# Shifted window attention: heads in four groups of three, first heads turned behind the projection, values and weighted values in 32-column tiles

## The chip, the cores and the metric

The kernel runs on one core of one Trainium2 chip. The metric is the device time of one execution in microseconds. Engines are called as in the profile: PE (matrix products and transposes), DVE (vector), ACT (scalar), POOL and SP (which issues most DMAs). Everything is fp32.

## The reference, cut to what matters

The input is 32 images of 96 channels by 16 x 16 positions. Two blocks follow each other; the change is in the first half of the first, the shifted window attention:

```python
xn = layernorm(x, norm1_g, norm1_b)                    # over the 96 channels of a position
xw = windows(roll(xn, (-4, -4)))                       # 4 windows of 8 x 8 = 64 positions per image
q, k, v = split(xw @ qkv_w + qkv_b)                    # 12 heads of 8 channels each
attn = softmax(q * 8**-0.5 @ k.T + rel_bias + mask)    # 64 x 64 per window and head
out = (attn @ v) @ proj_w + proj_b
x = x + unroll(out)                                    # the residual
x = x + gelu(layernorm(x) @ fc1_w + fc1_b) @ fc2_w + fc2_b
```

Then comes a second block (whole-image normalisation, grouped pointwise and 3 x 3 depthwise convolutions, attention between the 12 channels of a head, a final projection). The feed-forward part and the second block are the same before and after.

## The kernel before

Function `window_attention` works through the images one by one, and every engine runs its own program: a loop over steps, each with an order written out by hand, in which stages of several images stand together. In step t the engines work on images t to t + 4. `led_image_loop` runs four steps ahead of image 0, then the steps 0 to 31, in a loop of two steps per lap in the middle, and one step more behind the last image. Engines wait for each other by counting semaphores.

The stages of an image, in the order of its life:

- `turn_tokens` (PE): two transposes of the loaded image into `ps_tokens`, 128 positions a time. `measure` and `gather_spread` (DVE) take mean and variance, `inverse_deviation` and `scale` (ACT) scale the tokens, `turn_back` (PE) transposes them back into `ps_scaled`, `copy_normed` (ACT) copies them to `normed` in the order of the windows.
- `make_q_and_k` (PE): two products of 256 columns. `copy_q` (ACT) adds the bias. `copy_k` (DVE) adds the bias and spreads the keys into `k_blocks`: the keys once for each head of a group, with all channels but those of that head set to zero by `head_mask`. Heads stand in three groups (`NG`) of four (`GROUP`), 32 channels a group.
- `make_v` (PE): per window two products of 64 rows of output (64 columns of the array), `copy_v` (ACT) copies them to `v_blocks`, where each head has a ninth column of ones.
- For each of the two pairs of windows (p = 0, 1): `score` (PE) multiplies 64 queries with 256 columns of `k_blocks`, three groups and two windows; `add_bias` and `find_peak` (DVE); `subtract_peak` (POOL); `exponent` (ACT); `turn` (PE), six transposes; `copy_turned` (ACT).
- `weigh` (PE): probabilities times values, 12 products with 64 columns of the array and 54 moving columns: 18 are those of two heads, and the 36 behind them are written again by the next products (the last ones meet zero columns kept for this). The ones give the sum. `weigh_heads` (DVE) divides, `turn_heads` (PE) transposes, `copy_ot` (ACT) copies to `out_t`.
- `project` (PE) and `add_residual` (DVE), into `stream`.

The order in step t on PE is: project(t-1), turn_heads(t, 0), make_q_and_k(t+2), weigh(t, 1), turn(t+1, 0), score(t+2, 0), turn_heads(t, 1), turn_back(t+3), make_v(t+2), weigh(t+1, 0), score(t+2, 1), turn_tokens(t+4), turn(t+1, 1). On DVE: gather_spread, copy_k(t+2), weigh_heads(t, 1), add_residual(t-1), add_bias and find_peak(t+2, 0), weigh_heads(t+1, 0), add_bias(t+2, 1), measure(t+4), find_peak(t+2, 1). On ACT: copy_ot(t, 0), exponent(t+1, 0), copy_q(t+2), inverse_deviation and scale(t+3), copy_turned(t+1, 0), copy_ot(t, 1), exponent(t+1, 1), copy_normed(t+3), copy_v(t+2), copy_turned(t+1, 1).

PSUM has eight banks: three for the scores (q and k lie behind the scores of groups 0 and 1), two for the turned probabilities, one for the weighted values and turned heads (`ps_out`), `ps_a` for tokens and scaled tokens, `ps_b` for values and projection.

Ahead of the loop DVE and PE fold the norm's gain and bias into the weights (`prepare`, `fold_q_k_v`); PE runs products of zeros between (`fill`). SP loads the constants in two lists. In the last steps the tokens of the first eight chunks of the feed-forward part are turned (`turn_first`).

## Time and profile before

| | us |
|---|---|
| median of 3 timed runs (lowest, highest) | 508.53 (503.3, 512.01) |
| the profiled execution's own time | 499.01 |
| its span, first to last instruction | 497.2 |
| busy in the span: PE, DVE, ACT, POOL | 481.4, 369.7, 293.8, 195.7 |
| granted TensorE clock, mean | 0.994 |

The profiled execution is a single one, and its time is lower than the three timed runs. Busy times overlap. A PE that counts as busy need not be at its peak, since matmuls are pipelined and their ends are modelled. In the rows, "x24" is the count of instructions merged into one row, and an fp32 product counts as two matmuls, a transpose as one. Row starts are in us from the span's start. PEld are PE's weight loads.

### The profile page before, as it was taken

The page shows a single profiled execution, that of the slowest core. Times are in us where ns is not written, and L with a number is a line of the kernel's source. Part 1 is how long each engine was busy: PE and PEld are TensorE (multiplying, and loading weights), DVE is VectorE, ACT ScalarE, POOL GpSimd, SP SyncE. Part 2 cuts the span into 40 slices and gives each one's busy share as a digit, 9 for nine tenths or more (in the row PEclk, how much of TensorE's full clock was granted, in tenths as well). Part 3 has the DMA queues.
Part 4 walks back from the last instruction along what each step waited for, and adds up shares of the span by engine and source line. Part 5 has one row for each costly group of instructions (what it writes and reads, how often), then busy time and mean ns, then how long its engine had stood idle before and what let it go on. Part 6 is the DMA issues. An engine that isn't in the chain of part 4 may idle for free. (4 is left out here: it accounts for less than half of the span.)

```text
span 497.2 us, 22898 instructions
## 1 busy us (share of the span) xinstructions
PE 481.4 (97%) x8834; PEld 308.6 (62%) x8834; DVE 369.7 (74%) x1013; ACT 293.8 (59%) x743; POOL 195.7 (39%) x238
## 2 busy tenths in 40 slices
PE   8999999999999999999879999989999999999995
PEld 7767777777777777777644443335656565565652
DVE  2699999999999999999875463575765565656453
ACT  2577787778877787777665443433434444444431
POOL 8544434434443434443452542253344323233200
PEclk9999999999999999999999999999999999999999
DMA  4211011111111011100013232386444444443401
GB/s 81 69 36 33 21 28 50 32 24 24 32 32 29 19 32 32 32 16 3 2 40 97 51 81 66 96 213 140 121 116 110 114 120 117 106 123 104 126 21 32
DMA packets 41179, 32.54 MB, mean 65 GB/s; under 512 B 19240, under 2 KB 36776, under 8 KB 41128
## 3 DMA queue, kind: packets, MB, share of 16 engines
q1 hardware_dynamic: 36872, 25.36, 20.0%
q0 software_dynamic: 3584, 5.72, 5.3%
q10 hardware_dynamic: 672, 0.75, 0.5%
q8 instruction: 36, 0.59, 0.5%
q14 instruction: 15, 0.12, 0.1%
HBM read 18.36 MB, written 7.13 MB: 51 GB/s over the span
## 5 line engine op out<-in xcount | busy, mean ns | idle before, releaser
L380 POOL TENSOR_TENSOR scores<-scores,peak 128x768 f32<-128x768 f32 x64 | 94.2, 1472 | 128.3 <-DVE peak L560 128.3
L1043 POOL DMA_DIRECT2D x_stack<-padded_x x96 | 52.3, 548 | 91.9 <-PE ps_hidden L1563 70.6
L443 ACT COPY probs_t<-ps_probs 128x768 f32<-128x768 f32 x64 | 51.1, 798 | 40.4 <-PE ps_probs L707 40.3
L552 DVE TENSOR_TENSOR scores<-ps_scores,bias 128x768 f32<-128x768 f32 x64 | 61.3, 957 | 5.4 <-PE ps_scores L697 3.6
L560 DVE TENSOR_REDUCE peak<-scores 128x12 f32<-128x768 f32 x64 | 61.0, 953 | 2.4
L720 PE MATMUL ps_out<-v_blocks,probs_t 128*64 128x54 f32 x1536 | 57.2, 224 | 1.0 <-ACT out_t L448 0.9
L720 PEld LDWEIGHTS ps_out<-v_blocks,probs_t 128*64 128x64 f32 x1536 | 50.2, 138 | 12.3 <-issue 12.2
L437 ACT ACTIVATE scores<-scores 128x768 f32<-128x768 f32 x64 | 54.2, 847 | 1.5 <-POOL scores L380 1.5
L707 PE MATMUL ps_probs<-ident,scores 128*128 128x128 f32 x384 | 54.3, 277 | 0.0
L1563 PE MATMUL ps_turn<-x_stack,conv_w 40*32 40x256 f32 x1536 | 48.8, 379 | 1.6 <-DMA x_stack<-padded_x 1.6
L1563 PE MATMUL ps_hidden<-x_stack,conv_w 40*32 40x256 f32 x1536 | 49.5, 379 | 0.2 <-issue 0.2
L1151 ACT ACTIVATE hidden<-ps_hidden,fc_b_folded 128x512 f32<-128x512 f32 x44 | 26.6, 688 | 30.1 <-PE ps_hidden L1480 30.1
L697 PE MATMUL ps_scores<-k_blocks,q_sb 32*64 32x256 f32 x768 | 43.1, 399 | 0.9 <-issue 0.9
L707 PEld LDWEIGHTS ps_probs<-ident,scores 128*128 128x128 f32 x384 | 41.6, 140 | 2.8 <-issue 0.8
L539 DVE SCALAR_TENSOR_TENSOR k_blocks<-ps_scores,b_k,head_mask 96x1024 f32<-96x1024 f32 x32 | 40.6, 1269 | 2.5 <-PE ps_scores L675 2.5
L1170 ACT COPY qk_sb<-ps_turn 128x512 f32<-128x512 f32 x32 | 18.7, 586 | 38.4 <-PE ps_turn L1563 38.4
L1563 PEld LDWEIGHTS ps_turn<-x_stack,conv_w 40*32 40x32 f32 x1536 | 26.2, 105 | 21.5 <-issue 14.2
L1406 DVE TENSOR_REDUCE peak<-ps_hidden 128x2 f32<-128x24 f32 x32 | 5.8, 183 | 40.2 <-PE ps_hidden L1593 40.2
L1480 PE MATMUL ps_hidden<-normed,fc_sliced 32*128 32x512 f32 x264 | 31.4, 604 | 2.1 <-PEq L149 1.7
L1175 ACT COPY v_sb<-ps_hidden 128x512 f32<-128x512 f32 x32 | 18.8, 586 | 23.9 <-PE ps_hidden L1563 23.9
L1496 PE MATMUL ps_y<-hidden,fc 128*32 128x512 f32 x288 | 32.8, 595 | 0.0
L1563 PEld LDWEIGHTS ps_hidden<-x_stack,conv_w 40*32 40x32 f32 x1536 | 26.7, 105 | 8.6 <-issue 0.7
(157 smaller groups left out, 847.6 us busy)
## 6 DMA issues: line engine op xcount, KB each, us to landing
x_stack<-padded_x POOLq DMA_DIRECT2D x96, 54.0 KB, 2.7
x_stack<-padded_x SPq DMA_DIRECT2D x96, 54.0 KB
padded_x<-x_pad SPq DMA_DIRECT2D x26, 121.5 KB, 2.6
x_sliced<-stream SPq DMA_DIRECT2D x48, 64.0 KB, 2.0
stream<-y_sliced SPq DMA_DIRECT2D x48, 64.0 KB, 2.1
out<-out_sb SPq DMA_DIRECT2D x32, 96.0 KB, 2.0
x_now<-in_x SPq DMA_DIRECT2D x32, 72.0 KB, 1.8
stream<-in_x SPq DMA_DIRECT2D x32, 72.0 KB, 1.9
```

Source lines behind the costliest of these rows:

```text
L380: nc.gpsimd.tensor_tensor(sc, sc, peak[:, par, p, :].unsqueeze(2).to_broadcast((128, HEADS, WN)), ALU.subtract).then_inc(s["shifted"], 1)
L437: nc.scalar.activation(scores[:, par, p, :], scores[:, par, p, :], ACT.Exp).then_inc(s["probs_ready"], 1)
L443: nc.scalar.copy(probs_t[:, :], ps_turned).then_inc(s["turned_copied"], 1)
L539: nc.vector.scalar_tensor_tensor(out=k_blocks[:, :, :], in0=ps_k.unsqueeze(1).to_broadcast((C, GROUP, N)), scalar=b_k[:, 0:1], in1=head_ma ...
L552: nc.vector.tensor_tensor(scores[:, par, p, :].rearrange("p (g c) -> p g c", g=NG), ps_scores[:, :, 0:GROUP * WN], bias[:, p, :].rearrange ...
L560: nc.vector.tensor_reduce(peak[:, par, p, :], scores[:, par, p, :].rearrange("p (h m) -> p h m", m=WN), AX_X, ALU.max).then_inc(s["peak_re ...
L697: mm = nc.tensor.matmul(ps_scores[64 * w:64 * w + 64, g, 0:GROUP * WN], q, k, start=True, stop=True, skip_group_check=True)
L707: mm = nc.tensor.transpose(ps_turned[:, q * 128:(q + 1) * 128], scores[:, par, p, q * 128:(q + 1) * 128], ident[:, :])
L720: mm = nc.tensor.matmul(ps_out[64 * top:64 * top + 64, 0, q * 2 * VC:(q + 3) * 2 * VC], probs_t[:, q * 128 + 64 * top:q * 128 + 64 * top + ...
L1043: engine.dma_start(x_stack[64 * half + i * HC:64 * half + (i + 1) * HC, slot, :, :], rows).then_inc(landed[slot], 16)
L1496: mm = nc.tensor.matmul(ps_y[32 * r:32 * r + 32, n % 2, :], w["fc2"][:, h, 32 * c:32 * c + 32], hidden[:, g % 2, r, h, :], start=(h == 0), ...
L1563: mm = nc.tensor.matmul(ps[32 * k:32 * k + 32, r, :], conv_w[rows, kind, j, k, :], grid(x_stack[rows, slot, k, :], PADW)[:, :, j:j + W], s ...
```

## The change

- Heads stand in four groups of three. A group has 24 channels, padded to 32 rows with zeros (`w_qk`, `b_q`, `b_k`, `head_mask` and `cols_qk` get the padded form), and the scores have a bank for each of the four groups, 192 columns in each. `copy_k` writes 128 x 768 elements, where it wrote 96 x 1024.
- Tokens, scaled tokens, values and projection share one bank, `ps_ab`: tokens and values one region, scaled tokens and projection the other. New waits keep them apart: `turn_tokens` waits for copy_v of the image before, `turn_back` for a residual, `project` for copy_normed.
- `make_v` and `weigh` use tiles of 32 columns of the array: four products where two stood. `weigh` moves 18 columns, without the 36 that were written again, and `v_blocks` loses its zero columns.
- project(t) and turn_heads(t+1, 0) stand at the end of step t, ahead of turn_tokens(t+4) and turn(t+1, 1), where they stood behind these at the start of the next step. copy_ot(t+1, 0) goes ahead of copy_turned(t+1, 1) on ACT; add_residual(t) goes between measure(t+4) and find_peak(t+2, 1) on DVE. The step behind the last image is dropped.
- In the setup three loads leave SP's first list, eight small ones are issued by ACT ahead of its table load, behind two clears by POOL. The folded weights are copied by two instructions, and the folded biases of q and k are made group by group (`fold_q_k_v`, not shown).

```diff
...
-GROUP = 4
+GROUP = 3
+GROUP_C = GROUP * HD
+GROUP_COLS = GROUP * WN
...
-    step(B, B // 2, 0)
 def image_loop(engine, step, tail=1, lead=1, between=None, start=0):
...
-    head_mask = sb("head_mask", [C, GROUP])
+    head_mask = sb("head_mask", [128, GROUP])
-    w_qkv = sb("w_qkv", [C, 3 * C])
+    w_qk = sb("w_qk", [C, 2, NG, 32])
+    w_v = sb("w_v", [C, C])
-    b_q = sb("b_q", [C, 1])
-    b_k = sb("b_k", [C, 1])
+    cols_qk = sb("cols_qk", [128, 2])
+    b_q = sb("b_q", [128, 1])
+    b_k = sb("b_k", [128, 1])
...
-    q_sb = sb("q_sb", [C, N])
-    k_blocks = sb("k_blocks", [C, GROUP, N])
-    v_blocks = sb("v_blocks", [128, 2, PAIRS, 2, HP + 2, 2, VC])
+    q_sb = sb("q_sb", [128, N])
+    k_blocks = sb("k_blocks", [128, GROUP, N])
+    v_blocks = sb("v_blocks", [128, 2, PAIRS, 2, HP, 2, VC])
...
-    ps_a = bank("ps_a")
-    ps_b = bank("ps_b")
-    ps_tokens = ps_a[:, 0, 0:2 * C].rearrange("p (h c) -> p h c", c=C)
-    ps_scaled = ps_a[0:C, 0, N:2 * N]
+    ps_ab = bank("ps_ab")
+    ps_tokens = ps_ab[:, 0, 0:2 * C].rearrange("p (h c) -> p h c", c=C)
+    ps_scaled = ps_ab[0:C, 0, 2 * C:2 * C + N]
-    ps_q, ps_k = (ps_scores[0:C, g, GROUP * WN:GROUP * WN + N] for g in range(2))
-    ps_v = ps_b[:, 0, 0:2 * C].rearrange("p (w q d) -> p w q d", w=2 * PAIRS, d=HD)
-    ps_proj = ps_b[0:C, 0, 0:N]
+    ps_q, ps_k = (ps_scores[:, g, GROUP_COLS:GROUP_COLS + N] for g in range(2))
+    ps_v = ps_ab[:, 0, 0:2 * C].rearrange("p (w q d) -> p w q d", w=2 * PAIRS, d=HD)
+    ps_proj = ps_ab[0:C, 0, 2 * C:2 * C + N]
...
-    FIRST, SECOND = 8, 7
+    FIRST, SECOND = 5, 7
+    GROUPED = 2 * NG
...
-                 *((cols[:, 2 + k:3 + k], a["L0_conv_qkv_b"][k * C:(k + 1) * C].rearrange("(c a) -> c a", a=1))
-                   for k in range(3)),
-                 (head_mask[:, :], a["c_head_mask"]))
+                 (cols[:, 4:5], a["L0_conv_qkv_b"][2 * C:3 * C].rearrange("(c a) -> c a", a=1)))
...
     def _(pool):
+        nc.gpsimd.memset(head_mask[:, :], 0.0).then_inc(group_cleared, 1)
+        nc.gpsimd.memset(cols_qk[:, :], 0.0).then_inc(group_cleared, 1)
...
+        act.wait_ge(group_cleared, 2)
+        for g in range(NG):
+            rows, channels = slice(32 * g, 32 * g + GROUP_C), slice(GROUP_C * g, GROUP_C * (g + 1))
+            act.dma_start(cols_qk[rows, :], a["L0_conv_qkv_b"][0:2 * C].rearrange("(k c) -> c k", k=2)[channels, :],
+                          allow_slow_non_contiguous=True).then_inc(grouped_in, 16)
+            act.dma_start(head_mask[rows, :], a["c_head_mask"][0:GROUP_C, 0:GROUP]).then_inc(grouped_in, 16)
         def step(t, half, par):
-            if real(t):
-                copy_ot(t, 0, par)
             if is_image(t, B - 1):
...
             if is_image(t, B - 2):
             if real(t + 1):
+                copy_ot(t + 1, 0, 1 - par)
             if is_image(t, B - 2):
...
-                                    ps_scores[:, :, 0:GROUP * WN],
+                                    ps_scores[:, :, 0:GROUP_COLS],
...
         def add_residual(t, half, par):
-            dve.wait_ge(stream_in[1 - par], half * 32 if par == 0 else (half + 1) * 32)
+            dve.wait_ge(stream_in[par], (half + 1) * 32)
...
-            nc.vector.tensor_tensor(b_q[:, :], ps_out[0:C, 0, 0:1], cols[:, 2:3], ALU.add).then_inc(set_up, 1)
-            nc.vector.tensor_tensor(b_k[:, :], ps_out[0:C, 0, 1:2], cols[:, 3:4], ALU.add).then_inc(set_up, 1)
+            dve.wait_ge(grouped_in, 16 * GROUPED)
+            nc.vector.tensor_tensor(b_q[:, :], ps_out[:, 0, 0:1], cols_qk[:, 0:1], ALU.add).then_inc(set_up, 1)
+            nc.vector.tensor_tensor(b_k[:, :], ps_out[:, 0, 1:2], cols_qk[:, 1:2], ALU.add).then_inc(set_up, 1)
...
+            nc.vector.tensor_copy(w_qk[:, :, :, 0:GROUP_C].rearrange("c k g i -> c (k g) i"),
+                                  ps_folded[:, 0:2 * C].rearrange("c (g i) -> c g i", i=GROUP_C)).then_inc(centred, 1)
+            nc.vector.tensor_copy(w_v[:, :], ps_folded[:, 2 * C:3 * C]).then_inc(centred, 1)
         def step(t, half, par):
             if real(t + 3):
...
             if is_image(t, B - 2):
-            if real(t - 1):
-                add_residual(t - 1, half, par)
             if is_image(t, B - 2):
             if is_image(t, B - 1):
...
             if real(t + 4):
+            if real(t):
+                add_residual(t, half, par)
             if real(t + 2):
+        nc.vector.memset(w_qk[:, :, :, :], 0.0).then_inc(blanked, 1)
...
         def turn_tokens(t, half, par):
-            need(pe, s["scaled_ready"], t * 2)
+            need(pe, s["v_copied"], (t - 1) * 2)
         def turn_back(t):
+            need(pe, s["residual_done"], t - 3)
...
         def make_q_and_k(t):
             if is_image(t, 0):
-                pe.wait_ge(centred, 1)
+                pe.wait_ge(centred, 2)
-            nc.tensor.matmul(ps_q, w_qkv[:, 0:C], normed[:, :], start=True, stop=True,
+            nc.tensor.matmul(ps_q, w_qk[:, 0, :, :].rearrange("c g i -> c (g i)"), normed[:, :], start=True, stop=True,
-            nc.tensor.matmul(ps_k, w_qkv[:, C:2 * C], normed[:, :], start=True, stop=True,
+            nc.tensor.matmul(ps_k, w_qk[:, 1, :, :].rearrange("c g i -> c (g i)"), normed[:, :], start=True, stop=True,
         def make_v(t):
-            heads = w_qkv[:, 2 * C:3 * C].rearrange("c (q e d) -> c q e d", e=2, d=HD)
+            heads = w_v[:, :].rearrange("c (q e d) -> c q e d", e=2, d=HD)
-                for e in range(2):
-                    mm = nc.tensor.matmul(ps_v[64 * e:64 * e + 64, window, :, :], normed[:, window * WN:(window + 1) * WN],
-                                          heads[:, :, e, :], start=True, stop=True, skip_group_check=True)
+                for quarter in range(4):
+                    at = window * WN + 32 * (quarter % 2)
+                    mm = nc.tensor.matmul(ps_v[32 * quarter:32 * quarter + 32, window, :, :], normed[:, at:at + 32],
+                                          heads[:, :, quarter // 2, :], start=True, stop=True, skip_group_check=True)
         def score(t, p):
...
-                    mm = nc.tensor.matmul(ps_scores[64 * w:64 * w + 64, g, 0:GROUP * WN], q, k, start=True, stop=True,
+                    mm = nc.tensor.matmul(ps_scores[64 * w:64 * w + 64, g, 0:GROUP_COLS], q, k, start=True, stop=True,
...
-                for top in range(2):
-                    mm = nc.tensor.matmul(ps_out[64 * top:64 * top + 64, 0, q * 2 * VC:(q + 3) * 2 * VC],
-                                          probs_t[:, q * 128 + 64 * top:q * 128 + 64 * top + 64],
-                                          v_blocks[:, par, p, top, q:q + 3, :, :].rearrange("p q e c -> p (q e c)"),
+                for quarter in range(4):
+                    rows = slice(32 * quarter, 32 * quarter + 32)
+                    mm = nc.tensor.matmul(ps_out[rows, 0, q * 2 * VC:(q + 1) * 2 * VC],
+                                          probs_t[:, q * 128 + 32 * quarter:q * 128 + 32 * quarter + 32],
+                                          v_blocks[:, par, p, quarter // 2, q, :, :].rearrange("p e c -> p (e c)"),
...
         def project(t, par):
+            pe.wait_ge(s["normed_ready"], up_to(t + 3) * PAIRS)
...
         def step(t, half, par):
-            if real(t - 1):
-                project(t - 1, 1 - par)
-            if real(t):
-                turn_heads(t, 0)
             if is_image(t, B - 2):
...
             if real(t + 2):
+            if real(t):
+                project(t, par)
+            if real(t + 1):
+                turn_heads(t + 1, 0)
             if real(t + 4):
             if is_image(t, -3):
```

## Rows read from the trace of the kernel before

**Rows 1.** Windows: length, busy us of PE, PEld, DVE, ACT, POOL (instructions), granted clock, DMA.

```profile
10.00:20.00 10.00, 10.00 (x104) 8.16 (x103) 5.60 (x13) 2.72 (x10) 8.11 (x12) 0.83 0.29 59
100.00:140.00 40.00, 40.00 (x642) 29.43 (x630) 38.64 (x79) 31.78 (x85) 16.20 (x11) 1.00 0.12 28
```

**Rows 2.** Timeline of one step: start us, us, engine, line, operation, [idle before <-releaser].

```profile
160.79 0.85 ACT L437 ACTIVATE scores<-scores 128x768 f32<-128x768 f32 x1
...
161.46 1.26 DVE L539 SCALAR_TENSOR_TENSOR k_blocks<-ps_scores,b_k,head_mask 96x1024 f32<-96x1024 f32 x1
...
162.89 0.67 PE L697 MATMUL ps_scores<-k_blocks,q_sb 32*64 32x256 f32 x12
...
163.00 0.80 ACT L443 COPY probs_t<-ps_probs 128x768 f32<-128x768 f32 x1
163.19 0.48 DVE L577 SCALAR_TENSOR_TENSOR stream<-ps_b,b_proj,stream 96x256 f32 x1
...
163.74 0.96 DVE L552 TENSOR_TENSOR scores<-ps_scores,bias 128x768 f32<-128x768 f32 x1
163.85 0.26 ACT L448 COPY out_t<-ps_out 96x128 f32<-96x128 f32 x1
...
164.46 0.88 PE L720 MATMUL ps_out<-v_blocks,probs_t 128*64 128x54 f32 x24
...
165.05 0.68 ACT L432 COPY v_blocks<-ps_b 64x192 f32<-64x192 f32 x2
...
165.26 0.67 PE L697 MATMUL ps_scores<-k_blocks,q_sb 32*64 32x256 f32 x12
...
165.87 0.39 PE L659 MATMUL ps_a<-ident,x_now 96*128 96x96 f32 x2
...
166.09 0.82 PE L707 MATMUL ps_probs<-ident,scores 128*128 128x128 f32 x6
...
166.75 0.60 PE L736 MATMUL ps_b<-out_t,w_proj 96*96 96x256 f32 x2
166.95 0.80 ACT L443 COPY probs_t<-ps_probs 128x768 f32<-128x768 f32 x1 [1.21 <-PE ps_probs L707]
...
166.99 0.42 DVE L524 BATCH_NORM_STATS2 token_stats<-ps_a 128x6 f32<-128x96 f32 x2
...
167.18 0.27 PE L729 MATMUL ps_out<-ident,heads_out 128*96 128x128 f32 x1
...
167.34 0.59 PE L673 MATMUL ps_scores<-normed,w_qkv 96*96 96x256 f32 x2
...
167.64 0.26 ACT L448 COPY out_t<-ps_out 96x128 f32<-96x128 f32 x1
...
168.50 1.28 DVE L539 SCALAR_TENSOR_TENSOR k_blocks<-ps_scores,b_k,head_mask 96x1024 f32<-96x1024 f32 x1
```

**Rows 3.** Timeline, copies of the keys of images 2 and 31; 28 stand between them.

```profile
27.94 1.25 DVE L539 SCALAR_TENSOR_TENSOR k_blocks<-ps_scores,b_k,head_mask 96x1024 f32<-96x1024 f32 x1
...
231.49 1.28 DVE L539 SCALAR_TENSOR_TENSOR k_blocks<-ps_scores,b_k,head_mask 96x1024 f32<-96x1024 f32 x1 [0.27 <-PE ps_scores L675]
```

**Rows 4.** Groups of instructions, the Gram product: busy us, mean ns of one.

```profile
L1593 PE MATMUL ps_hidden<-tokens 128*32 128x12 f32 x1024 | 14.1, 182 | 0.2 <-DVE tokens L1401 0.2
```

**Rows 5.** Timeline of the drain: a copy by ACT and the product that waits for it.

```profile
243.91 0.27 ACT L448 COPY out_t<-ps_out 96x128 f32<-96x128 f32 x1
...
244.28 0.91 PE L720 MATMUL ps_out<-v_blocks,probs_t 128*64 128x54 f32 x24 [0.93 <-ACT out_t L448]
```

**Rows 6.** Timeline of the setup, 0 to 8 us.

```profile
0.86 1.28 ACT L450 ACT_TABLE_LOAD   x1 [0.86 <-PEq L1682]
...
5.53 0.43 SPq L330 DMA_DIRECT2D head_mask<-in_c_head_mask  x1
5.83 0.30 ACT L398 ACTIVATE log_var<-spread,eps 128x2 f32<-128x2 f32 x1 [3.69 <-DVE spread L534]
...
7.67 0.37 DVE L582 TENSOR_SCALAR w_gained<-w_in,cols 96x288 f32<-96x288 f32 x1 [1.94 <-DMA head_mask<-in_c_head_mask]
```

More of the change, by code:

```diff
@@ L257, in window_attention @@
     ps_ot = ps_out[0:C, 0, 384:512]
-    first_homes = [ps_scores[:, 0, :], ps_scores[:, 1, :], ps_scores[:, 2, :], ps_a[:, 0, :]]
+    first_homes = [ps_scores[:, g, :] for g in range(NG)]
     ps_fold = [ps_probs[:, c % 2, 0:HID] for c in range(SLICES)]
-    ps_fold_b = ps_a[:, 0, BLOCKS * C:BLOCKS * C + HT]
+    ps_fold_b = ps_scores[:, 3, BLOCKS * C:BLOCKS * C + HT]
     ps_slices = [ps_probs[:, 1 - c % 2, :] for c in range(SLICES)]
@@ L265, in window_attention @@
     consts_in = sem("consts_in")
+    group_cleared = sem("group_cleared")
+    grouped_in = sem("grouped_in")
     second_in = sem("second_in")
@@ L538, in copy_k @@
             need(dve, s["scores_ready"], t * 2)
-            nc.vector.scalar_tensor_tensor(out=k_blocks[:, :, :], in0=ps_k.unsqueeze(1).to_broadcast((C, GROUP, N)),
+            nc.vector.scalar_tensor_tensor(out=k_blocks[:, :, :], in0=ps_k.unsqueeze(1).to_broadcast((128, GROUP, N)),
                                            scalar=b_k[:, 0:1],
-                                           in1=head_mask[:, :].unsqueeze(2).to_broadcast((C, GROUP, N)),
+                                           in1=head_mask[:, :].unsqueeze(2).to_broadcast((128, GROUP, N)),
                                            op0=ALU.add, op1=ALU.mult).then_inc(s["k_copied"], 1)
@@ L589, in prepare @@
             dve.wait_ge(folded, 1)
-            nc.vector.tensor_copy(w_qkv[:, :], ps_folded).then_inc(centred, 1)
+            dve.wait_ge(blanked, 2)
+            nc.vector.tensor_copy(w_qk[:, :, :, 0:GROUP_C].rearrange("c k g i -> c (k g) i"),
+                                  ps_folded[:, 0:2 * C].rearrange("c (g i) -> c g i", i=GROUP_C)).then_inc(centred, 1)
+            nc.vector.tensor_copy(w_v[:, :], ps_folded[:, 2 * C:3 * C]).then_inc(centred, 1)
         def step(t, half, par):
@@ L638, in fold_q_k_v @@
             pe.wait_ge(consts_in, 16 * FIRST)
-            for k in range(3):
-                nc.tensor.matmul(ps_out[0:C, 0, k:k + 1], w_in[:, k * C:(k + 1) * C], cols[:, 1:2],
-                                 start=True, stop=True, skip_group_check=True).then_inc(pe_set, 1)
+            for k in range(2):
+                for g in range(NG):
+                    at = k * C + g * GROUP_C
+                    mm = nc.tensor.matmul(ps_out[32 * g:32 * g + 32, 0, k:k + 1], w_in[:, at:at + 32], cols[:, 1:2],
+                                          start=True, stop=True, skip_group_check=True)
+                mm.then_inc(pe_set, 1)
+            nc.tensor.matmul(ps_out[0:C, 0, 2:3], w_in[:, 2 * C:3 * C], cols[:, 1:2],
+                             start=True, stop=True, skip_group_check=True).then_inc(pe_set, 1)
         def fold_v():
```

## The prediction

> **What bounds the kernel now.** I read the windows first. Between 100 and 140 us PE is busy 40.00 of 40 us and DVE 38.64, ACT 31.78, POOL 16.20 [rows 1]. Two engines are full at once, so the share of busy time can't say which one a saving has to come from. The timeline of one step tells more [rows 2]: copy_k of one image starts at 161.46 and of the next at 168.50, so this step takes 7.04 us, and from the copy of image 2 at 27.94 to that of image 31 at 231.49 there are 29 steps of 7.02 us [rows 3]. The change touches these steps, the setup ahead of them and the drain behind; the phases that follow the attention have the same instructions before and after.
>
> In that step the reader is to follow three chains. On PE each group begins when the one before has left the array (score at 162.89, weigh at 164.46, score at 165.26, tokens at 165.87, turn at 166.09, project at 166.75, heads at 167.18, q at 167.34): PE waits for nobody. On DVE the gaps are under 0.1 us: copy_k, reciprocal and weighted heads, residual (163.19), bias (163.74), peak, reciprocal and heads, the second bias, statistics (166.99), peak, spread, copy_k (168.50). ACT runs without a pause from one copy_turned behind the second turn to the end of copy_v at 165.73, and is then idle 1.21 us until turn has given it the next such copy_turned at 166.95.
>
> **The change part by part.**
>
> *32-column tiles on PE.* Weigh goes from 24 matmuls to 48, make_v from 16 to 32, each score from 12 to 16 (an fp32 product is two instructions). Weigh now holds PE from 164.46 to 165.26, 0.80 us, or 33 ns a matmul [rows 2]. The nearest row in the new form is the Gram product of the last phase, 128 rows by 32 columns with 12 moving: 1024 in 14.1 us, 14 ns each [rows 4]. 48 x 14 = 0.66 us, so two weighs give back about 0.3 us, bounds 0 and 0.7 (the upper if four tiles cost what two did: 0.80 / 2 each, with its start). make_v gains the same share of a smaller group, 0.1. A score has 192 moving columns in place of 256 in each of two passes: 64 columns x 2 x 2 passes over 2.4 GHz (the granted clock is 1.00 [rows 1]) is 0.11 us less, 4 matmuls more at the Gram row's 14 ns cost 0.06, so 0.67 becomes about 0.62. In all PE loses some 0.5 to 0.8 us of 7.02 and stops being the bound. Whether that shortens the step depends on who is second, and DVE is 0.25 us behind.
>
> The Trainium skill speaks against this part: "TensorEngine Tiling (Array Packing)", Performance Considerations, says that a matmul has some 60 cycles of overhead, that one moving column costs as much as 60, and that tiling should not be taken from a dimension that is already small; weigh goes from 54 moving columns to 18. By its figure (25 ns at 2.4 GHz, an estimate) a weigh would take 1.2 us. The Gram row is at 14 ns with 12 columns, so the trace does not agree where tiles of one shape follow each other.
>
> *copy_k.* 96x1024 took 1.26 us, and the residual, the same operation on 96x256, 0.48 [rows 2]. On the line through both, 128x768 takes 1.00: 0.26 us less on DVE per step.
>
> *The residual moves.* It runs now between the weighted heads and the bias addition, from 163.19 to 163.67, while DVE waits for the score anyway: the score can start only when copy_k has ended at 162.72, and its result lets the bias start at 163.74. So its 0.48 us is free today. In the change it stands between the statistics and the second peak, where DVE has no wait; there it costs 0.51 (itself and a gap of 0.03). The hole that it leaves stays open: copy_k's end to the score's start is 0.17, the score 0.62, its end to the bias 0.18, together 0.97 in place of 1.02, with almost 0.5 of it idle (reciprocal and heads stay in it).
>
> *DVE's chain, summed.* Now: copy_k 1.26, to the bias 1.02, bias to statistics 3.25 (163.74 to 166.99), statistics to the next copy_k 1.51; together 7.04. After: 1.00 + 0.97 + 3.25 + 1.51 + 0.51 = 7.24. Bounds: with the score at 0.56 (no charge for the four) and its start 0.10 behind copy_k (as short as the wait shown at the drain [rows 5]) it is 7.11; with an unchanged score 7.29.
>
> *One PSUM bank for tokens, values, normalised tokens and projection.* This adds waits. turn_tokens(t+4) waits for copy_v(t+2), since both write one region; project(t) waits for copy_v(t+2) and copy_normed(t+3); turn_back waits for a residual of the step before, which is long done. Today turn_tokens starts at 165.87, only 0.14 us behind copy_v, and the projection stands behind turn. After the change project, turn_heads(t+1, 0), turn_tokens and turn(t+1, 1) queue on PE behind copy_v, and ACT's next work, copy_turned, is behind turn. That closes a loop between ACT and PE, and each link has its price in [rows 2]. ACT: copy_turned to the next exponent 0.69 (166.95 to 167.64; the copy of the first heads that stands there now moves into the idle time ahead of copy_turned); exponent 160.79 to the end of copy_v 165.73, 4.94, of which copy_turned to copy_ot took 0.85 where 0.69 is enough; turn_heads came late there, and with a shorter weigh and score it should not, so 4.78. PE: 0.10 from ACT's end to the matmul [rows 5], project 0.43 (166.75 to 167.18), heads 0.16 (167.18 to q at 167.34), tokens 0.22, turn to copy_turned 0.86 (166.09 to 166.95). Sum 0.69 + 4.78 + 0.10 + 0.43 + 0.16 + 0.22 + 0.86 = 7.24 us. Bounds: 7.15 with the links tighter by what the rows round away, 7.40 if the late turn_heads stays. DVE waits in this loop too: its statistics need the tokens, which come about 1.1 us behind copy_v, where DVE's own chain has it ready at about the same time.
>
> So two chains stand at 7.24, and PE's own work far below. With the same rounding the step shown is 7.04 where the mean is 7.02, so I take 7.22: a step grows by 0.20 us, 29 steps by 5.8.
>
> *Moved copy_ot and turn_heads.* The first heads are turned earlier and copied in ACT's idle time, so weigh(t, 1) no longer waits for them. PE's queue was full then, so this is worth nothing by itself. The cover is ACT's wait for turn, some 1.7 us after the change; without it 0.16 would return.
>
> *Setup.* Three DMAs leave SP's first list. Each holds SP 0.43 us and a small gap (head_mask, the last, at 5.53), and the first vector work on the weights waited for that last load until 7.67 [rows 6]. Some 1.4 us less on that path. Eight small loads go on ACT's queue ahead of its table load (0.86 to 2.14 today): at SP's 0.43 each they end near 4.5, the table near 5.8, and ACT's first operation was at 5.83, so nothing or little is lost there; DVE waits for them only where it adds the biases, behind the work on the weights. POOL clears two small tiles first, 0.2 us. I take -1.2, bounds -1.5 and +1.
>
> *Drain.* The step behind the last image disappears, but its projection stands behind the same turned chunks as before; shorter weighs give perhaps -0.5 (0 to -1).
>
> Sum: +5.8 - 1.2 - 0.5 = +4.1 us on the profiled execution's 499.0 (span 497.2 and 1.8 around it), 503.1. The three timed runs lie higher, at 508.5 median (503.3 to 512.0); I add the difference to it: 512.6.
>
> **The rivals.**
>
> *DVE's shorter sum sets the step.* If the score's answer were there when DVE asks, a step would lose copy_k's 0.26: 29 x 0.26 = 7.5, with setup and drain -9.2, 499.3. For it: DVE is full and its work does shrink. Against it: the bias can't start before score, score not before copy_k, and after the move only 0.5 us of work is left to cover 0.95.
>
> *The ACT loop binds harder (slower).* If turn_heads(t, 1) still comes late for copy_ot (0.16) and PE needs 0.15 more to start behind copy_v, the step is 7.24 + 0.31 = 7.55, by the mean 7.53: 29 x 0.51 = 14.8, less 1.7, 521.6. It decides as soon as the loop passes DVE's chain of 7.24, and nothing overlaps there: project, heads, tokens and turn are in series between two ACT operations. For it: copy_ot did wait in the rows shown. Against it: PE has 0.5 us more air.
>
> *The narrow tiles don't get cheaper.* If a matmul of weigh costs 33 ns at 32 columns as at 64, 48 take 1.58, and PE's step, full today, becomes 7.02 + 2 x 0.78 = 8.58 and somewhat more for make_v: 29 x 1.56 = 45, 552 or above. The Gram row speaks against it. The Trainium skill's rule on tiling a small dimension, named above, points this way.
>
> *The clock falls.* Weigh streams 18 columns in place of 54 and PE will stand idle in each step. The granted clock was 0.83 over 10 to 20 us although PE counted as busy throughout [rows 1], so a busy PE alone doesn't hold it. At the lower of its two levels (1.2 for 2.4 GHz) for good, PE's step of some 6.4 us would go towards 10, 90 us in all, 600. Against it: 1.00 in the steps shown, with the same transposes and projections as after.
>
> **How the numbers follow.** Forecast (step 7.05 to 7.38, time 508 to 517) 0.59; ACT loop 0.24; DVE's sum 0.10; narrow tiles 0.02; clock 0.03; setup or another thing that I don't see 0.02. The loop's case lies between 517 and 525, so a part of it is within 2% (2% is 10 us here, about what these runs can tell from no change). Over 2% slower: two thirds of the loop's case and the two large ones, 0.21; over 2% faster, under 498.4: half of DVE's case at most, 0.06; within: 0.73. The range for 8 in 10 takes in the bounds of the chains and of setup: 504 to 520.
>
> **What would show it.** Right: copy_k starts some 7.2 us apart; the first bias addition of a step has an idle time of about 0.4 us before it with the score as releaser; copy_k near 1.0 us; the weigh group under 0.75 us; PE busy well under 40 of 40 us; project starting about 0.1 us behind copy_v's end, and copy_turned idle some 1.7 us with turn as releaser. Wrong: DVE without an idle time (then the step is near 6.8), or steps above 7.35 with the bias's wait larger than 0.6 us (then ACT's loop binds alone), or weighs above 1 us.

## The result and the profile after

The changed kernel takes 513.24 us where the kernel before, timed beside it, takes 509.5 (medians); the ratio is 1.017 [1.011, 1.023]. Two later series gave 1.010 [1.002, 1.017] and 1.011 [1.005, 1.017]: about 1% slower. Executions of one kernel fall into a faster and a slower state, and the ratio compares the faster ones alone, so it is not the quotient of the medians. The profiled execution took 507.43 us with a span of 505.6, against 499.01 and 497.2.

The span first, cut where [rows 3] cut it. Timeline of the changed kernel, copies of the keys of images 2 and 31:

```profile
33.86 0.99 DVE L549 SCALAR_TENSOR_TENSOR k_blocks<-ps_scores,b_k,head_mask 128x768 f32<-128x768 f32 x1
...
241.60 1.02 DVE L549 SCALAR_TENSOR_TENSOR k_blocks<-ps_scores,b_k,head_mask 128x768 f32<-128x768 f32 x1
```

Setup ends at 33.86 in place of 27.94 (+5.9); 29 steps take 207.74 in place of 203.55 (+4.2, 7.16 each); from there to the end of the span it is 264.0 in place of 265.7 (-1.7). Together +8.4.

Windows of the changed kernel, to set beside [rows 1] (length, busy us of PE, PEld, DVE, ACT, POOL with instructions, granted clock, DMA):

```profile
100.00:140.00 40.00, 35.86 (x1043) 26.32 (x1044) 35.48 (x79) 31.10 (x85) 16.61 (x12) 1.00 0.12 25
```

Nobody is full any more. PE, which had no gap in 40 us, now stands idle for 4.1 of them, and DVE for 4.5 where it was 1.4. The costliest groups of the page (busy us, mean ns of one, idle before them and what ended it):

```profile
L562 DVE TENSOR_TENSOR scores<-ps_scores,bias 128x768 f32<-128x768 f32 x64 | 61.3, 957 | 19.8 <-PE ps_scores L720 19.8
L744 PE MATMUL ps_out<-v_blocks,probs_t 128*32 128x18 f32 x3072 | 39.4, 187 | 4.3 <-ACT probs_t L448 1.3
L549 DVE SCALAR_TENSOR_TENSOR k_blocks<-ps_scores,b_k,head_mask 128x768 f32<-128x768 f32 x32 | 31.5, 985 | 4.1 <-PE ps_scores L697 4.0
L453 ACT COPY out_t<-ps_out 96x128 f32<-96x128 f32 x64 | 16.9, 265 | 29.1 <-PE ps_out L753 29.1
```

DVE waits 19.8 us ahead of the bias additions, all of it for the score; ACT 29.1 ahead of copy_ot, for the turned heads. Two steps of the timeline show how (start, us, engine, line, [idle before <-releaser]), beside [rows 2]:

```profile
148.39 0.85 ACT L442 ACTIVATE scores<-scores 128x768 f32<-128x768 f32 x1
...
149.15 0.98 DVE L549 SCALAR_TENSOR_TENSOR k_blocks<-ps_scores,b_k,head_mask 128x768 f32<-128x768 f32 x1
...
150.23 0.59 PE L720 MATMUL ps_scores<-k_blocks,q_sb 32*64 32x192 f32 x16
...
151.00 0.96 DVE L562 TENSOR_TENSOR scores<-ps_scores,bias 128x768 f32<-128x768 f32 x1 [0.44 <-PE ps_scores L720]
...
151.65 0.60 PE L744 MATMUL ps_out<-v_blocks,probs_t 128*32 128x18 f32 x48
...
152.20 0.58 PE L720 MATMUL ps_scores<-k_blocks,q_sb 32*64 32x192 f32 x16
152.48 0.70 ACT L437 COPY v_blocks<-ps_ab 64x192 f32<-64x192 f32 x2
...
153.28 0.64 PE L761 MATMUL ps_ab<-out_t,w_proj 96*96 96x256 f32 x2 [0.49 <-ACT v_blocks L437]
...
153.76 0.28 PE L753 MATMUL ps_out<-ident,heads_out 128*96 128x128 f32 x1
...
153.87 0.33 PE L679 MATMUL ps_ab<-ident,x_now 96*128 96x96 f32 x2
...
154.04 0.82 PE L730 MATMUL ps_probs<-ident,scores 128*128 128x128 f32 x6
154.07 0.26 ACT L453 COPY out_t<-ps_out 96x128 f32<-96x128 f32 x1 [0.89 <-PE ps_out L753]
154.33 0.43 DVE L534 BATCH_NORM_STATS2 token_stats<-ps_ab 128x6 f32<-128x96 f32 x2
...
154.89 0.80 ACT L448 COPY probs_t<-ps_probs 128x768 f32<-128x768 f32 x1 [0.56 <-PE ps_probs L730]
...
155.07 0.48 DVE L587 SCALAR_TENSOR_TENSOR stream<-ps_ab,b_proj,stream 96x256 f32 x1 [0.31 <-DVE token_stats L534]
...
155.59 0.85 ACT L442 ACTIVATE scores<-scores 128x768 f32<-128x768 f32 x1
...
156.49 0.98 DVE L549 SCALAR_TENSOR_TENSOR k_blocks<-ps_scores,b_k,head_mask 128x768 f32<-128x768 f32 x1
...
158.34 0.96 DVE L562 TENSOR_TENSOR scores<-ps_scores,bias 128x768 f32<-128x768 f32 x1 [0.44 <-PE ps_scores L720]
...
159.65 0.69 ACT L437 COPY v_blocks<-ps_ab 64x192 f32<-64x192 f32 x2
...
161.51 0.42 DVE L534 BATCH_NORM_STATS2 token_stats<-ps_ab 128x6 f32<-128x96 f32 x2
162.08 0.48 DVE L587 SCALAR_TENSOR_TENSOR stream<-ps_ab,b_proj,stream 96x256 f32 x1
...
162.74 0.85 ACT L442 ACTIVATE scores<-scores 128x768 f32<-128x768 f32 x1
...
163.50 0.98 DVE L549 SCALAR_TENSOR_TENSOR k_blocks<-ps_scores,b_k,head_mask 128x768 f32<-128x768 f32 x1
```

The hole ahead of the bias (0.44, at 151.00 and 158.34) stands in both steps, and project starts 0.10 behind copy_v's end (152.48 + 0.70 = 153.18, then 153.28). But copy_k to copy_k is 7.34 in the first and 7.01 in the second, and so on in turn, 7.175 in the mean. Nothing in the prediction has two kinds of step; the experiments explain it.

### The profile page after: what moved, and what is told of

Its sections match the earlier page's. It is cut to its first block and busy times, and to the rows that moved or that the text cites. A ratio compares the mean times of both kernels' runs of the same rounds, so it can differ in the third digit from the quotient of the medians.

```text
span 505.6 us, 27496 instructions
## 1 busy us (share of the span) xinstructions
PE 471.1 (93%) x11150; PEld 300.5 (59%) x11150; DVE 357.5 (71%) x1015; ACT 292.7 (58%) x743; POOL 195.4 (39%) x240
## 5 line engine op out<-in xcount | busy, mean ns | idle before, releaser
L562 DVE TENSOR_TENSOR scores<-ps_scores,bias 128x768 f32<-128x768 f32 x64 | 61.3, 957 | 19.8 <-PE ps_scores L720 19.8
L744 PEld LDWEIGHTS ps_out<-v_blocks,probs_t 128*32 128x32 f32 x3072 | 34.4, 110 | 16.8 <-issue 11.0
L744 PE MATMUL ps_out<-v_blocks,probs_t 128*32 128x18 f32 x3072 | 39.4, 187 | 4.3 <-ACT probs_t L448 1.3
L720 PE MATMUL ps_scores<-k_blocks,q_sb 32*64 32x192 f32 x1024 | 38.3, 353 | 3.6 <-issue 2.7
L1588 PEld LDWEIGHTS ps_turn<-x_stack,conv_w 40*32 40x32 f32 x1536 | 26.1, 105 | 21.7 <-issue 14.6
L549 DVE SCALAR_TENSOR_TENSOR k_blocks<-ps_scores,b_k,head_mask 128x768 f32<-128x768 f32 x32 | 31.5, 985 | 4.1 <-PE ps_scores L697 4.0
L453 ACT COPY out_t<-ps_out 96x128 f32<-96x128 f32 x64 | 16.9, 265 | 29.1 <-PE ps_out L753 29.1
```

What stands on the lines that cost most here:

```text
L562: nc.vector.tensor_tensor(scores[:, par, p, :].rearrange("p (g c) -> p g c", g=NG), ps_scores[:, :, 0:GROUP_COLS], bias[:, p, :].rearrange ...
L720: mm = nc.tensor.matmul(ps_scores[64 * w:64 * w + 64, g, 0:GROUP_COLS], q, k, start=True, stop=True, skip_group_check=True)
L744: mm = nc.tensor.matmul(ps_out[rows, 0, q * 2 * VC:(q + 1) * 2 * VC], probs_t[:, q * 128 + 32 * quarter:q * 128 + 32 * quarter + 32], v_bl ...
L1588: mm = nc.tensor.matmul(ps[32 * k:32 * k + 32, r, :], conv_w[rows, kind, j, k, :], grid(x_stack[rows, slot, k, :], PADW)[:, :, j:j + W], s ...
```

## The experiments

The steps are read from each run's timeline; totals are single runs unless a ratio is given.

**Which chain sets the step?** Three kernels from the changed one. The first makes the residual short:

```diff
-            dst = stream[:, bass.ds(t * N, N)]
-            nc.vector.scalar_tensor_tensor(out=dst, in0=ps_proj, scalar=b_proj[:, 0:1], in1=dst,
+            dst = stream[:, bass.ds(t * N, 16)]
+            nc.vector.scalar_tensor_tensor(out=dst, in0=ps_proj[:, 0:16], scalar=b_proj[:, 0:1], in1=dst,
```

> The residual adds 16 of 256 columns (the rest of the projection is left out of the stream), so it holds DVE about 0.23 us instead of 0.48, and nothing else changes. A step of the changed kernel is 7.16 us (copies of the keys of images 2 and 31, 29 steps). If DVE's chain sets the step, it loses all of it: about 6.91. If the loop between ACT and PE sets it: 7.16, and DVE only waits 0.25 longer for the tokens. If both stand at the same length, as forecast: a small part, 7.05 to 7.12.

501.1 us; steps of 6.86 and 7.46 in turn, 7.142 over 29. The second gives ACT another order:

```diff
-            if real(t + 1):
-                exponent(t + 1, 1, 1 - par)
             if real(t + 3):
                 copy_normed(t + 3)
             if real(t + 2):
                 copy_v(t + 2, par)
+            if real(t + 1):
+                exponent(t + 1, 1, 1 - par)
```

> On ACT copy_normed and copy_v go ahead of the second exponent of a step, so that the projection and the tokens no longer wait for the 0.85 us of that exponent; turn then waits for it instead, at the same time as PE projects. If the loop between ACT and PE sets the step, it shrinks by 0.3 to 0.5 us: 6.7 to 6.9. If DVE's chain does: 7.16 as now. If both are equally long: 7.05 to 7.12, no more than what the loop was above DVE's chain.

512.49 us (its setup ended at 33.79, see below); steps of 7.18 and 7.01, 7.075 over 29. Each edit alone gives next to nothing. The third does both:

> The changed kernel with both of the first edits: 16 columns of the residual (the rest of the projection left out) and copy_normed and copy_v ahead of the second exponent. Each alone left the step at 7.14 and 7.08. If two chains of nearly equal length stand side by side, cutting both lets the step fall by much more than the sum of the two (0.02 and 0.09): to 6.8 to 6.9. If a third thing sets the step, such as PE or POOL: 7.05 as before, the sum of both.

Steps of 7.06 and 6.77, 6.911 over 29: 0.25 less than the changed kernel's 7.163, more than 0.02 and 0.09 together. (The total, 512.9 us, has low-clock stretches outside the steps and is not used.) So two chains stand side by side, and each hides what the other gives up. The pairs then give the length of each by itself. With ACT's order changed, the timeline of DVE shows no wait for tokens in either step:

```profile
152.47 0.42 DVE L534 BATCH_NORM_STATS2 token_stats<-ps_ab 128x6 f32<-128x96 f32 x2
153.20 0.48 DVE L587 SCALAR_TENSOR_TENSOR stream<-ps_ab,b_proj,stream 96x256 f32 x1 [0.31 <-DVE token_stats L534]
...
159.64 0.42 DVE L534 BATCH_NORM_STATS2 token_stats<-ps_ab 128x6 f32<-128x96 f32 x2
160.21 0.48 DVE L587 SCALAR_TENSOR_TENSOR stream<-ps_ab,b_proj,stream 96x256 f32 x1
```

That is DVE's chain alone: (7.18 + 7.01) / 2 = 7.09. The two steps differ by where the residual starts behind the statistics, 0.73 or 0.57. In the changed kernel's records of DVE's sequencer two register operations and a semaphore event of the residual's own waits stand in that gap in the longer step (154.80, 154.90, 154.96), one register operation in the other (161.97); the loop body holds two steps, and only one of them seems to work out the wait's value there. In the changed kernel the longer step has a wait for the tokens besides: bias to statistics is 3.33 us there (151.00 to 154.33) and 3.17 in the shorter. These 0.16 and the 0.16 of the residual make up the 0.33 between the two steps, to a hundredth. With the short residual it is the other chain that is alone. From its longer step:

```profile
157.13 0.96 DVE L562 TENSOR_TENSOR scores<-ps_scores,bias 128x768 f32<-128x768 f32 x1 [0.68 <-PE ps_scores L720]
...
160.59 0.43 DVE L534 BATCH_NORM_STATS2 token_stats<-ps_ab 128x6 f32<-128x96 f32 x2 [0.20 <-PE ps_ab L679]
161.33 0.23 DVE L587 SCALAR_TENSOR_TENSOR stream<-ps_ab,b_proj,stream 96x16 f32 x1 [0.31 <-DVE token_stats L534]
```

DVE now waits 0.20 for the tokens, which PE turns behind copy_v, and 0.24 more than before for the score; with the register work's 0.16 that is the 0.60 between the two steps. So DVE follows the loop of ACT and PE, (6.86 + 7.46) / 2 = 7.16. In the changed kernel DVE is 7.09, the loop 7.16, the step 7.175: the loop binds, by 0.07. The pace of copy_v agrees. In the changed kernel its starts are 7.17 apart (152.48 and 159.65) and 7.16 to 7.19 in the steps around, though copy_k alternates between 7.34 and 7.01; with ACT's order changed they alternate as copy_k does, 7.18 and 7.01, since DVE binds there.

**What are the narrow tiles worth?** The kernel before with the 32-column tiles of make_v and weigh, and nothing else:

```diff
-                for top in range(2):
-                    mm = nc.tensor.matmul(ps_out[64 * top:64 * top + 64, 0, q * 2 * VC:(q + 3) * 2 * VC],
...
+                for quarter in range(4):
+                    rows = slice(32 * quarter, 32 * quarter + 32)
+                    mm = nc.tensor.matmul(ps_out[rows, 0, q * 2 * VC:(q + 1) * 2 * VC],
```

> The kernel before with the 32-column tiles of make_v and weigh alone: 48 matmuls of 18 columns and 32 of 48, three groups, two banks and the old order. PE's groups get shorter by some 0.7 us a step in all (weigh from 0.80 to about 0.5 each). If PE set the step before and DVE is 0.2 us behind it: a step of 6.80 to 6.90 for 7.02, a full DVE and 4 to 6 us less in the whole. If DVE was the bound already: 7.0. If narrow tiles cost as much per matmul as wide ones: 8.5.

496.26 us, 0.985 [0.974, 0.995]; step 6.85. Again with more rounds:

> The kernel before with only the 32-column tiles of the values and of the weighted values, once more and with more rounds: step 6.85, 0.980 to 0.990 of the kernel before, if the first ratio of 0.9845 held. Rival: the first was drawn by one slow setup of the kernel before, then 0.99 to 1.00 with the step still at 6.85.

496.84 us, 0.973 [0.970, 0.977]; step 6.85. It beats both kernels: PE's queue had cost 0.17 us of the step (7.02 to 6.85). The steps make 5.0 us of the gain, 1.0%. The second ratio also holds executions of the kernel before at a lower clock; in that series those with a mean granted clock of 0.988 or more took 495.8 us with this kernel (five) and 502.1 with the kernel before (four), 1.3% less. Windows of this kernel:

```profile
100.00:140.00 40.00, 38.70 (x1050) 26.37 (x1048) 38.96 (x82) 33.10 (x89) 17.03 (x12) 1.00 0.14 30
```

Timeline of its DVE around the hole:

```profile
151.65 0.48 DVE L577 SCALAR_TENSOR_TENSOR stream<-ps_b,b_proj,stream 96x256 f32 x1
...
152.11 0.96 DVE L552 TENSOR_TENSOR scores<-ps_scores,bias 128x768 f32<-128x768 f32 x1
```

PE has left 40.00, DVE is the bound, and its residual fills the time in which the score is made. Is it the width of the tile or the number of moving columns? The kernel before with 18 moving columns on its 64-column tiles:

> The kernel before, with weigh moving 18 columns in place of 54, still in tiles of 64 columns: 24 matmuls a weigh, the same weight loads. If the width of the tile (the weight load) sets the spacing of weigh's matmuls: weigh stays at 0.80 us and the step at 7.02. If the moving columns set it: weigh about 0.4 and the step 6.85, and then the narrow tiles had no part in the gain of the run with the tiles alone.

497.51 us; step 6.96, PE still 40.00 of 40. The groups of weigh, in the kernel before, in this one and in the one with narrow tiles (64 weighs each):

```profile
L720 PE MATMUL ps_out<-v_blocks,probs_t 128*64 128x54 f32 x1536 | 57.2, 224 | 1.0 <-ACT out_t L448 0.9
```

```profile
L720 PE MATMUL ps_out<-v_blocks,probs_t 128*64 128x18 f32 x1536 | 55.2, 211 | 1.0 <-ACT out_t L448 0.9
```

```profile
L722 PE MATMUL ps_out<-v_blocks,probs_t 128*32 128x18 f32 x3072 | 39.5, 187 | 1.0 <-ACT out_t L448 0.9
```

55.2 us with the columns cut, 39.5 with the tiles cut as well: twice the instructions in 0.72 of the time. The single records say the same: pairs of 64-column matmuls start 58 to 59 ns apart with 54 moving columns and with 18 (one gap of the latter is shorter), and four narrow ones take 35 to 38 ns together. So it is mostly the width of the tile; cutting the columns alone gave 0.06 of the 0.17 us.

**What does the move cost by itself?** On the kernel with narrow tiles, project, turn_heads, copy_ot and the residual are moved as in the change; the separate banks and the three groups of four stay as in the kernel before:

```diff
-            if real(t - 1):
-                add_residual(t - 1, half, par)
...
+            if real(t):
+                add_residual(t, half, par)
             if real(t + 2):
                 find_peak(t + 2, 1, par)
```

> The kernel with the narrow tiles alone, and the change of order on top: project and turn_heads ahead of turn_tokens and turn, copy_ot ahead of copy_turned, the residual between the statistics and the second peak. Groups stay three, banks two. Its step was 6.85 in the old order. If the residual's move opens a hole ahead of the bias on DVE: 1.25 + 0.97 + 3.25 + 1.51 + 0.51 = 7.4 to 7.5. If only the loop of ACT and PE behind copy_v counts: 7.15. If the order costs nothing and the shared bank did it: 6.85.

530.58 us; steps of 7.65 and 7.35, 7.50 where the clock is up (7.59 with one step of 11.27 in a low stretch). Rows of this kernel:

```profile
151.50 1.25 DVE L537 SCALAR_TENSOR_TENSOR k_blocks<-ps_scores,b_k,head_mask 96x1024 f32<-96x1024 f32 x1
...
153.69 0.96 DVE L550 TENSOR_TENSOR scores<-ps_scores,bias 128x768 f32<-128x768 f32 x1 [0.51 <-PE ps_scores L696]
...
155.92 0.64 PE L736 MATMUL ps_b<-out_t,w_proj 96*96 96x256 f32 x2 [0.35 <-ACT v_blocks L431]
...
156.71 0.26 ACT L447 COPY out_t<-ps_out 96x128 f32<-96x128 f32 x1 [0.94 <-PE ps_out L729]
...
157.54 0.80 ACT L442 COPY probs_t<-ps_probs 128x768 f32<-128x768 f32 x1 [0.56 <-PE ps_probs L706]
```

The move alone makes the step 0.65 longer. The loop of ACT and PE is there too, though tokens and values have separate banks: project waits for copy_v (155.92), and ACT stands idle 0.94 and 0.56 for the turned heads and the turned probabilities, as in the changed kernel (0.89 and 0.56). In the kernel before, values and projection already shared `ps_b` and project already waited for copy_v. So the loop comes with the new place of project, ahead of tokens and turn, and does not need the shared bank. The residual's 0.51 stands in a new place and 0.08 of register work with it; the hole that it left has 0.51 of idle time and is no shorter for it. In the changed kernel, with four groups of three and a copy_k of 0.98 for 1.25, the step is 7.175: half of the loss comes back.

**Can the residual go back?** Ahead of the first bias, everything else as changed; and the same with ACT's other order:

```diff
-            dve.wait_ge(stream_in[par], (half + 1) * 32)
+            dve.wait_ge(stream_in[1 - par], half * 32 if par == 0 else (half + 1) * 32)
+            dve.wait_ge(s["scaled_ready"], up_to(t + 4) * 2)
...
+            if real(t - 1):
+                add_residual(t - 1, half, par)
...
-            if real(t):
-                add_residual(t, half, par)
```

> The changed kernel with one part undone: the residual stands again between the weighted heads and the first bias addition (that of the image before, in the next step), and everything else of the change stays. Nothing is left out. Two chains side by side (my theory): DVE's chain falls by the residual's 0.5 us from 7.2 to about 6.7, but the loop of ACT and PE behind copy_v stays at about 7.1, so a step should take 7.10 to 7.17 as with the short residual (7.142 there), still in long and short pairs, and ACT should still be idle over 0.8 us ahead of copy_ot of the second heads. Rival, DVE's chain alone sets the step and the short residual disturbed something else: 6.7 to 6.85.

> The same with copy_normed and copy_v ahead of the second exponent on ACT as well, so both chains are shortened and nothing is left out. Theory of two chains: with DVE's near 6.7 and the loop of ACT and PE near 6.8 to 6.9 (6.911 with a short residual and this order), a step should take 6.80 to 6.92, a drop of over 0.25 from the changed kernel's 7.17, where the two edits alone give 0.03 and 0.09. Against the kernel before: 29 x -0.15 = -4 us and the drain's -1.7, about 500 to 503 where that takes 506. Against the kernel before with only the narrow tiles (6.845): about the same, so the move and the three groups would be worth nothing beside the tiles. Rival: if a third wait binds (PE's queue behind the second score), 7.0 to 7.1.

Both missed: 520.19 us, 1.025 [1.018, 1.032], step 7.505; and 523.21 us, 1.026 [1.022, 1.031], step 7.62. The rows put it down to the added wait. Tokens and projection share a bank, so the edit holds the residual until ACT has scaled the tokens of that bank. Groups of the first of the two:

```profile
L588 DVE SCALAR_TENSOR_TENSOR stream<-ps_ab,b_proj,stream 96x256 f32 (+1 forms) x32 | 15.3, 477 | 20.7 <-ACT scaled L412 20.0 <-DMA stream<-in_x 0.7
L689 PE MATMUL ps_ab<-ident,scaled 128*96 128x128 f32 x64 | 13.5, 293 | 14.6 <-DVE stream L588 14.6
```

DVE waits 20.0 us in 32 residuals for ACT, some 0.7 each, where the hole was 0.44; the bias starts 2.57 to 2.61 behind copy_k where it was 1.85; and PE's turn_back, which writes the residual's columns, waits 14.6 us for DVE. The misses say nothing against two chains, since a third wait was added to them. They show that with this wait the residual can't fill the hole; a version without it wasn't tried. The Trainium skill ("PSUM — Partial Sum Buffer", PSUM bank collisions raise a hardware error) says that two engines must not access one bank and quadrant at once, reads included; no run here shows it.

**Was the first profile a fair one?** The two kernels again, for their setup:

> The changed kernel once more, for the setup. In its first profile the copy of the keys of image 2 came at 33.9 us, where it came at 27.9 before, with PE's products in the setup at twice their length until about 28 us. If that belongs to the change, the copy comes near 34 again and the setup's products are slow again. If the clock's rise falls differently in every execution, the copy comes anywhere between 27 and 34. The step should be 7.16 within 0.03 either way.

507.05 us, 1.010; steady steps 7.35 and 7.01, copy_k of image 2 at 29.47.

> The kernel before, a second look at its setup. Step 7.02. If the clock's rise in the setup falls by chance, the copy of the keys of image 2 may come later than the 27.9 of the first look, up to 33; if the old setup holds the clock, near 26 to 28 again.

501.25 us, step 7.018, copy_k of image 2 at 29.77.

> The changed kernel a third time: steady steps in pairs of 7.35 and 7.01, mean 7.17 to 7.18. For the setup: copy_k of image 2 near 26 to 27 if TensorE's clock rises by 8 us and stays, near 29 to 30 with one low stretch behind the rise, near 34 with a rise at 28 us. Ratio 1.005 to 1.017: 1.010 or less if late rises are chance in both kernels, 1.015 or more if the changed setup brings them in most executions.

512.3 us, 1.011; steady steps 7.34 and 7.01, copy_k of image 2 at 26.58. The ratio lies between the two that would have decided. The steps come back to 0.01; the setup doesn't. A window of the first profile of the changed kernel, and products of PE ahead of and behind 28.7 us, where the clock rose:

```profile
10.00:20.00 10.00, 10.00 (x78) 8.12 (x82) 3.49 (x13) 1.43 (x5) 6.39 (x11) 1.00 0.24 50
```

```profile
17.86 0.94 PE L720 MATMUL ps_scores<-k_blocks,q_sb 32*64 32x192 f32 x16
...
26.90 1.49 PE L730 MATMUL ps_probs<-ident,scores 128*128 128x128 f32 x6
...
30.28 0.58 PE L720 MATMUL ps_scores<-k_blocks,q_sb 32*64 32x192 f32 x16
...
31.92 0.82 PE L730 MATMUL ps_probs<-ident,scores 128*128 128x128 f32 x6
```

The same score takes 0.94 and 0.58, the same transposes 1.49 and 0.82: the setup ran at the lower of the two levels (1.2 for 2.4 GHz) to its end, though PE counted as busy from 10 to 20 us without a pause. The granted clock of 1.00 in that window is not a reading: the first clock record of this profile stands at 28.7 us, and the level ahead of it is read from the durations. In the other profiles the clock was up by 8 us. Where it then stayed up through the setup, copy_k of image 2 stands at 26.24, 26.32 and 26.58 with the changed setup and at 26.45 with the old one (narrow tiles); with one early fall and rise at 28.59 to 29.47 and at 27.84 to 29.77. The late rise came in 2 of 8 profiles of the changed setup (values ahead of the exponent was the other) and in none of 6 of the old one; whether the change makes it likelier stays open.

## Why the prediction came out right, point by point

**The total.** +4.1 us was said; the medians differ by 3.7, 0.7 and 3.6, and the three ratios make it some 8.6, 4.8 and 5.4 of 502. The profiled executions differ by 8.4. That the sum came out so near is in part luck: the steps were put 1.6 us too high, and the 1.7 us that setup and drain were to give back do not show, so two errors cancel.

**The steps: +5.8 said, +4.2 measured.** The mechanism held, two chains of nearly one length, but neither is 7.24. The loop of ACT and PE, by the first step shown: copy_turned to exponent 0.70 (0.69 said), exponent to the end of copy_v 4.79 (4.78), to project 0.10 (0.10), project 0.48 (0.43), heads 0.11 (0.16), tokens 0.17 (0.22), turn to copy_turned 0.85 (0.86): 7.20, and 7.15 from that exponent to the next. It was said to be 7.24 with a bound of 7.15, and it is the one that binds. Its cause was read wrongly: the prediction closed it with the shared bank, but project waited for copy_v before as well, and the run with the move alone shows the same loop with separate banks. What the shared bank costs by itself no run shows. DVE's chain was 7.24 with a lower bound of 7.11, and is 7.09: copy_k to bias 1.85 for 1.97 (the score starts 0.10 behind copy_k, which was the bound's value, not the one taken), bias to statistics 3.17 for 3.25, statistics to copy_k 1.99 for 2.02; and 0.08 in the mean for the residual's register work in every second step, which the prediction didn't see. In the old place that work lay in the hole.

**The tiles on PE.** Weigh's start to the next score is 0.55 (151.65 to 152.20), 11.5 ns a matmul; 0.66 was taken from the Gram row [rows 4] with 0.40 as the lower bound. The score, 0.59 for 0.62. PE's own work fell by 0.6 (7.02 to 35.86 / 40 x 7.175 = 6.43; 0.5 to 0.8 said). The Trainium skill's rule that tiling should not be taken from a small dimension ("TensorEngine Tiling (Array Packing)", Performance Considerations) would have made weigh 1.2 us by the estimate of the prediction, which sets the 48 matmuls one behind the other; the trace does not agree (0.55 us), and the kernel with the tiles alone is the fastest measured here.

**copy_k** takes 0.985 (1.00 said), and **the hole** has 0.44 of idle time with the score as releaser (about 0.4 said). copy_turned's idle 1.7 came as 0.89 ahead of copy_ot and 0.56 behind it, 1.45, with the turned heads and turn as releasers.

**Setup: -1.2 said, +5.9 in the profile, 0 in like executions.** Here the step that failed is "some 1.4 us less on that path". SP's last load of the first list did issue at 4.12 in place of 5.53, and ACT's table load came at 4.59 without delaying the first Ln (5.88, where it was 5.83 [rows 6]), both as said. But the weights:

```profile
7.70 0.37 DVE L592 TENSOR_SCALAR w_gained<-w_in,cols 96x288 f32<-96x288 f32 x1 [1.96 <-DMA cols<-in_L_conv_qkv_b]
```

7.70 in place of 7.67. The loads of the changed kernel's setup (KB each, us from issue to landing):

```profile
cols_qk<-in_L_conv_qkv_b ACTq DMA_DIRECT2D x4, 0.2 KB
head_mask<-in_c_head_mask ACTq DMA_DIRECT2D x4, 0.3 KB
cols<-in_L_conv_qkv_b SPq DMA_DIRECT2D x1, 0.4 KB, 3.5
```

The last load now takes 3.5 us from issue to landing, where the last one before took 2.1; 4.12 + 3.5 is 5.53 + 2.1. A load of the same size issued at 4.12 us landed after 2.4 to 2.5 us in all six profiles with the old setup, and after 3.2 to 3.6 in all eight with the new. New around it are the eight loads that ACT issues from 1.03 to 4.56, and a load of the second image that follows sooner (4.59 for 6.00); no run varies either alone. Time of issue was counted and time to land was not. The Trainium skill ("DMA: Bandwidth & Descriptors", Issuing engines are not separate DMA queues) says that loads started by several engines run on the same DMA engines, and that a second issuer saves only the issuing; the trace agrees, with 3.5 us for 2.1. The 5.9 are the clock, which the prediction priced only as lost for good (the fourth rival) and not as late.

**Drain: -0.5 said, -1.7 in this pair.** Like executions run from 264.0 (this profile) to 266.15 (the changed kernel again) with the clock up, so neither number is shown.

**The rivals.** DVE's shorter sum did not set the step, because of the hole; with the residual left where it was and narrow tiles it nearly does (6.85, DVE 38.96 of 40). The loop didn't reach 7.55: copy_ot of the second heads starts without a wait. The narrow tiles did get cheaper. The granted clock stood at 1.00 from 100 to 140 us; no profile shows it down for good.

## What to carry to other kernels

When a step is moved on an engine that isn't the bound, ask what it was covering: the residual cost nothing between copy_k and the bias, and 0.5 us and a hole behind them. When two chains have one length, undo them together, since either alone shows nothing (0.02 and 0.09 against 0.25). A large change is best split by its parts: here one part alone was worth 1.0% by its steps and 1.5 to 2.7% by the two ratios, and the rest took more than it gave.

## What the runs showed of the hardware

- Four 32-column tiles side by side took 11.5 ns a matmul with 18 moving columns; two 64-column tiles took 0.80 us / 24 = 33 ns with 54 [rows 2], and hardly less with 18 (55.2 us in the group where 57.2 stood before). These figures hold the 0.14 to 0.15 us that pass between the last matmul of a weigh and the first of the score behind it, in either form.
- TensorE's clock rose at 6 to 8 us in most executions and at 28.6 or 28.7 in two, and fell again in some for 3.4 to 24 us, between 9 and 62 us, at 245 to 280 and at 331 to 379. Much of the spread between executions of one kernel goes with it: the kernel before took 499.0 to 502.6 us with a mean granted clock of 0.990 to 0.996, and 506 to 515 at 0.961 to 0.980. The falls near 250 stand in 7 of the 14 profiles and begin 14 to 23 us behind the copy of the last image's keys, where the attention runs out; the same stretch is run without a fall in the other seven, so what sets a fall off isn't shown.
- A load's time to land isn't its own: for a load of 0.4 KB issued at 4.12 us, 2.4 us became 3.5 where ACT issued eight small loads between 1.03 and 4.56 and the next large one followed at 4.59.
- Register work for a wait on a changing value stands in an engine's path like an instruction: 0.16 us here, with the semaphore event beside it.
